# A decoder block's expert stage: first table of tiles in three pieces, earlier pads, down product one tile sooner

## The reference, cut to what matters

```
x = x + attn(norm(x))            # returns its input plus the attention: 16 heads of 8
x = x + xattn(norm(x), ctx, ctx) # 16 heads of 64, rotary, causal window of 32
x = x + ffn(norm(x))             # below

logits = x_ @ router.T ; idx = argmax(logits)      # 8 experts, one per row
y  = down[idx] @ (silu(gate[idx] @ x_) * (up[idx] @ x_))
ys = shared expert, for every row
return y + ys
```

## Time and profile before

| what | value |
|---|---|
| median of three runs | 772.91 us |
| the profiled execution | 773.4 us |
| its span in the trace | 771.3 us |
| PE busy, share of the span | 740.5 us, 96% |
| DVE (VectorE) | 544.2 us, 71% |
| ACT (ScalarE) | 534.7 us, 69% |
| POOL (GpSimd) | 525.7 us, 68% |
| mean granted clock of PE | 0.986 |

### The profile page before, as it was taken

How to read it: one execution, slowest core, us unless ns; L and a number is a source line. 1 busy time by engine, 2 the same in 40 slices (tenths; PEclk the granted TensorE clock), 3 DMA queues, 4 the chain that set the end, 5 groups by cost and what they waited for, 6 DMA issues and landing times.

```text
span 771.3 us, 31550 instructions
## 1 busy us (share of the span) xinstructions
PE 740.5 (96%) x11799; PEld 603.4 (78%) x11799; DVE 544.2 (71%) x1401; ACT 534.7 (69%) x1943; POOL 525.7 (68%) x857
## 2 busy tenths in 40 slices
PE   7999999999999999999999999999999989998894
PEld 6778878888888888787888888888888868776563
DVE  3467777777777777688777777777777777657463
ACT  2367777777777777777777777777777757774362
POOL 5466677677777777777777777777777756474554
PEclk9999999999999999999999999999999989999898
DMA  6000000111111000000000000000000003015420
GB/s 242 9 9 9 29 27 28 34 38 37 38 37 38 13 17 25 23 17 24 24 24 24 24 17 14 17 17 17 17 17 10 11 1 97 10 52 182 119 82 21
DMA packets 23539, 28.74 MB, mean 37 GB/s; under 512 B 3416, under 2 KB 19676, under 8 KB 23392
## 3 DMA queue, kind: packets, MB, share of 16 engines
q1 hardware_dynamic: 19888, 18.55, 8.0%
q0 software_dynamic: 2784, 6.56, 2.5%
q10 hardware_dynamic: 720, 1.63, 0.6%
HBM read 16.82 MB, written 10.35 MB: 35 GB/s over the span
## 4 chain that ended last, share of the span: by engine, by line
PE 91%; DVE 2%; ACT 2%; issue 2%; DMA 1%; SPq 0%; POOL 0%; POOLq 0%; ACTq 0%; DVEq 0%
PE P L277 8%; PE P L312 8%; PE P L287 8%; PE P L297 7%; PE P L353 7%; PE P L339 6%; PE P L325 5%; PE P L229 5%; PE P L212 4%; PE P L371 4%; PE P L244 4%; PE P L418 4%; PE P L379 3%; PE P L252 2%; PE P L342 1%
## 5 line engine op out<-in xcount | busy, mean ns | idle before, releaser
L857 ACT ACTIVATE PX<-P,mx 128x128 f32<-128x128 f32 x512 | 183.6, 393 | 27.7 <-DVE mx L590 27.7
L1027 POOL TENSOR_TENSOR PX<-PX,mx 128x512 f32<-128x512 f32 x128 | 130.5, 1041 | 36.5 <-DVE mx L595 36.5
L590 DVE TENSOR_REDUCE mx<-P 128x4 f32<-128x512 f32 x128 | 81.2, 678 | 93.5 <-PE P L312 93.5
L857 ACT ACTIVATION_READ_ACCUMULATOR PX<-P,mx 128x1 f32 x512 | 119.3, 233 | 0.0
L866 ACT ACTIVATE PT<-P 128x512 f32<-128x512 f32 x128 | 70.0, 597 | 64.5 <-PE P L325 64.5
L973 POOL TENSOR_SCALAR st<-st 128x1 f32<-128x1 f32 x96 | 22.0, 229 | 105.9 <-DVE st L498 99.6
L1022 POOL TENSOR_TENSOR rq<-rq,tq 128x1024 f32<-128x1024 f32 x32 | 75.6, 2363 | 25.9 <-DVE rq L554 25.9
L529 DVE TENSOR_REDUCE nmf<-P 128x4 f32<-128x512 f32 x128 | 79.5, 683 | 13.8 <-PE P L212 13.8
L821 ACT ACTIVATE PS<-P 128x512 f32<-128x512 f32 x128 | 66.1, 602 | 28.4 <-PE P L233 28.4
L1017 POOL TENSOR_TENSOR rk<-rk,tk 128x1024 f32<-128x1024 f32 x32 | 75.5, 2360 | 1.1 <-DVE tk L554 1.1
L277 PE MATMUL P<-wvT,cxT 128*128 128x512 f32 x128 | 72.2, 646 | 0.0
(11 more groups left out here) (156 smaller groups left out, 1828.7 us busy)
## 6 DMA issues: line engine op xcount, KB each, us to landing
xrow<-z_xs SPq DMA_DIRECT2D x39, 136.0 KB, 2.1
ew<-in_ew SPq DMA_DIRECT2D x9, 384.0 KB, 3.3
z_xs<-c SPq DMA_DIRECT2D x8, 272.0 KB
x<-in_x SPq DMA_DIRECT2D x32, 64.0 KB, 1.7
cxT<-in_ctxT SPq DMA_DIRECT2D x31, 64.0 KB, 1.8
z_xs<-c SPq DMA_DIRECT2D x8, 136.0 KB, 3.1
out<-yst,xrow POOLq DMA_INDIRECT x39, 2.3
wk<-in_wk SPq DMA_DIRECT2D x1, 512.0 KB, 4.5
```

Source lines behind the costliest of these rows:

```text
L590: dve.tensor_reduce(mx[b % 3][:, 0, r, :], v3(bank(f"ds{r}")), AX.X, ALU.max, negate=True).then_inc(S["v_dm"][r], 1)
L857: t = act.activation(PX[(4 * b + r) % 6][:, c, :], p[:, c * 128:c * 128 + 128], ACT.Exp, bias=m[:, 0, r, c:c + 1], scale=1.0, accum_out=m[ ...
L1027: pool.tensor_tensor(X[:, :, :], X[:, :, :], mx[b % 3][:, 2, r, :].rearrange("p (h a) -> p h a", a=1).to_broadcast([128, 4, 128]), ALU.mul ...
```

## The change

Five things are changed.

- The table is cut into three functions. `table_sums` has the count of tiles and the sums, `table_experts` the experts and exg, `table_rows` the first rows and exr. For c = 0 only the sums stay in f_pos; table_experts(0) runs one period later between r_q3 and r_q1 (f_experts, s - 8), table_rows(0) later in that period between the d_max and r_k1 (f_rows). For c = 1 all three follow each other in f_pos.
- The number of tiles is now had by rounding: a large number is added, at which float32 has steps of 128, and taken off again, two operations on 8 numbers. The minimum is part of exg's operation, and in the second table the last addition part of exr's.
- The pads use the counts of batch 29 and are 384 rows long; batch 30's scatter waits for them. SP's first_r is called in the period of the last piece.
- In the last loop the down product and VectorE's sum are those of tile j - 3, and the loops are one iteration shorter.
- WARM has 13 idle products for ('nmt', 2) instead of 16.

```diff
--- before.py
+++ after.py
@@ -37,7 +37,7 @@
             xr0=4, xr1=5, xr2=2, xr3=2, xrt0=4, xrt1=5, xt0=3, xt1=0, xt2=2, xt3=7, xtt0=0, xy0=0, xy1=3, xy2=7,
             xy3=1, xyt0=6, xyt1=7)
 WARM = {('a', 0): 36, ('a', 1): 14, ('nmt', 0): 43, ('kE', 1): 13, ('cnt', 0): 13, ('qO', 0): 9, ('ds0', 0): 22,
-        ('cnt', 1): 19, ('nmt', 2): 16}
+        ('cnt', 1): 19, ('nmt', 2): 13}
 S0, PERIODS = 27, 45
 
 
@@ -383,7 +383,7 @@
 
             def f_pos(b):
                 until = [(S["v_pse"], b + 1)]
-                if b == NB - 2:
+                if b == NB - 3:
                     until.append((S["v_pad"], 1))
                 if b + 1 in (FIRST[1], NB):
                     until.append((S["v_cnt"], chunk(b) + 1))
@@ -478,11 +478,11 @@
                 batch(d_t, s - 5, 0)
                 batch(b_s, s - 3)
                 tile(x_hT, s - 35, 0)
-            for j in range(TILE0[1], NT + 4):
+            for j in range(TILE0[1], NT + 3):
                 last(x_tr, j)
                 last(x_hT, j - 3)
                 last(x_up, j - 1)
-                last(x_dn, j - 4)
+                last(x_dn, j - 3)
 
         @block.vector
         def _(dve):
@@ -642,29 +642,29 @@
                 dve.tensor_tensor(f[:, 0:8], bank("pos")[:, 0:8], OH[:, b, :], ALU.mult).then_inc(S["v_own"], 1)
                 dve.wait_ge(S["v_own"], own())
                 dve.tensor_reduce(f[:, 8:9], f[:, 0:8], AX.X, ALU.add).then_inc(S["v_pse"], 1)
-                if b == NB - 2:
+                if b == NB - 3:
                     dve.scalar_tensor_tensor(out=padr[:, :], in0=experts, scalar=float(128 * CAP), in1=bank("pos")[:, 8:16],
                                              op0=ALU.mult, op1=ALU.add).then_inc(S["v_pad"], 1)
                 if b + 1 in (FIRST[1], NB):
                     dve.tensor_copy(cnt[:, 0:8], bank("pos")[:, 8:16]).then_inc(S["v_cnt"], 1)
-                    tile_table(chunk(b))
-
-
-
-
-            def tile_table(c):
-                t0, T = TILE0[c], TILES[c]
-                n = [CHUNKS[0], NB][c]
-                own_tiles, incl, w = cnt[:, 8:16], cnt[:, 16:24], cnt[:, 24:32]
-
-                done, after, upto, before = cnt[:, 32:40], cnt[:, 33:41], cnt[:, 41:49], cnt[:, 40:48]
-                cm = cmpb[:, 0:8 * n].rearrange("p (e j) -> p e j", e=NE)
+                    table_sums(chunk(b))
+                if b + 1 == NB:
+                    table_experts(1)
+                    table_rows(1)
+
+
+
+
+            own_tiles, incl, w = cnt[:, 8:16], cnt[:, 16:24], cnt[:, 24:32]
+
+            done, after, upto, before = cnt[:, 32:40], cnt[:, 33:41], cnt[:, 41:49], cnt[:, 40:48]
+
+            def table_sums(c):
+
                 dve.wait_ge(S["v_cnt"], c + 1)
-                dve.tensor_tensor(cm, cnt[:, 0:8].rearrange("p (e a) -> p e a", a=1).to_broadcast([128, NE, n]),
-                                  steps[:, 1 - c:1 - c + n].rearrange("p (a j) -> p a j", a=1).to_broadcast([128, NE, n]),
-                                  [ALU.is_ge, ALU.is_gt][c]).then_inc(S["v_own"], 1)
+                dve.tensor_scalar(own_tiles, cnt[:, 0:8], [-63.5, 63.5][c], 1.5 * 2.0 ** 30, ALU.add, ALU.add).then_inc(S["v_own"], 1)
                 dve.wait_ge(S["v_own"], own())
-                dve.tensor_reduce(own_tiles, cm, AX.X, ALU.add).then_inc(S["v_own"], 1)
+                dve.tensor_scalar(own_tiles, own_tiles, -1.5 * 2.0 ** 30, 1.0 / 128, ALU.add, ALU.mult).then_inc(S["v_own"], 1)
                 dve.wait_ge(S["v_own"], own())
                 if c == 1:
                     dve.tensor_tensor(own_tiles, own_tiles, done, ALU.subtract).then_inc(S["v_own"], 1)
@@ -672,12 +672,16 @@
                 c2 = cmpb[:, 0:64].rearrange("p (e f) -> p e f", e=NE)
                 dve.tensor_tensor(c2, own_tiles.rearrange("p (a f) -> p a f", a=1).to_broadcast([128, NE, NE]),
                                   tri[:, :, :], ALU.mult).then_inc(S["v_own"], 1)
-                dve.wait_ge(S["v_own"], own())
-                dve.tensor_reduce(incl, c2, AX.X, ALU.add).then_inc(S["v_own"], 1)
                 dve.tensor_scalar(w, own_tiles, -1.0, float(CAP), ALU.mult, ALU.add).then_inc(S["v_own"], 1)
                 own()
                 dve.wait_ge(S["v_own"], own())
+                dve.tensor_reduce(incl, c2, AX.X, ALU.add).then_inc(S["v_own"], 1)
+                own()
+
+            def table_experts(c):
+                t0, T = TILE0[c], TILES[c]
                 c3 = cmpb[:, 0:8 * T].rearrange("p (j e) -> p j e", e=NE)
+                dve.wait_ge(S["v_own"], mine[0])
                 dve.tensor_tensor(c3, incl.rearrange("p (a e) -> p a e", a=1).to_broadcast([128, T, NE]),
                                   tiles[:, 0:T].rearrange("p (j a) -> p j a", a=1).to_broadcast([128, T, NE]),
                                   ALU.is_le).then_inc(S["v_own"], 1)
@@ -697,21 +701,32 @@
                 dve.tensor_reduce(exf[:, 0:T], c3, AX.X, ALU.add).then_inc(S["v_own"], 1)
                 own()
                 dve.wait_ge(S["v_own"], own())
-                dve.tensor_scalar(exf[:, 0:T], exf[:, 0:T], 7.0, None, ALU.min).then_inc(S["v_own"], 1)
                 dve.tensor_tensor(c3, c3, w.rearrange("p (a e) -> p a e", a=1).to_broadcast([128, T, NE]),
                                   ALU.mult).then_inc(S["v_own"], 1)
+                dve.tensor_scalar(exg[:, t0:t0 + T], exf[:, 0:T], 7.0, float(EW), ALU.min, ALU.mult).then_inc(S["v_ex"], 1)
                 own()
-                dve.wait_ge(S["v_own"], own())
-                dve.tensor_scalar(exg[:, t0:t0 + T], exf[:, 0:T], float(EW), None, ALU.mult).then_inc(S["v_ex"], 1)
+
+            def table_rows(c):
+                t0, T = TILE0[c], TILES[c]
+                c3 = cmpb[:, 0:8 * T].rearrange("p (j e) -> p j e", e=NE)
+                dve.wait_ge(S["v_own"], mine[0])
                 dve.tensor_reduce(exf[:, MOST:MOST + T], c3, AX.X, ALU.add).then_inc(S["v_own"], 1)
                 dve.wait_ge(S["v_own"], own())
                 dve.tensor_tensor(exf[:, MOST:MOST + T], exf[:, MOST:MOST + T], tiles[:, 0:T], ALU.add).then_inc(S["v_own"], 1)
                 dve.wait_ge(S["v_own"], own())
                 if c == 1:
-                    dve.tensor_scalar(exf[:, MOST:MOST + T], exf[:, MOST:MOST + T], cnt[:, 32:33], None,
-                                      ALU.add).then_inc(S["v_own"], 1)
-                    dve.wait_ge(S["v_own"], own())
-                dve.tensor_scalar(exr[:, t0:t0 + T], exf[:, MOST:MOST + T], 128.0, None, ALU.mult).then_inc(S["v_ex"], 1)
+                    dve.tensor_scalar(exr[:, t0:t0 + T], exf[:, MOST:MOST + T], cnt[:, 32:33], 128.0, ALU.add,
+                                      ALU.mult).then_inc(S["v_ex"], 1)
+                else:
+                    dve.tensor_scalar(exr[:, t0:t0 + T], exf[:, MOST:MOST + T], 128.0, None, ALU.mult).then_inc(S["v_ex"], 1)
+
+            def f_experts(b):
+                if b + 1 == FIRST[1]:
+                    table_experts(0)
+
+            def f_rows(b):
+                if b + 1 == FIRST[1]:
+                    table_rows(0)
 
             def x_gate(j):
                 T, p = xth[j % 3], bank(xbank("xg", j))
@@ -740,6 +755,7 @@
                 tile(x_gate, s - 36, 3)
                 batch(b_max, s - 4, 3)
                 batch(r_q3, s - 5)
+                batch(f_experts, s - 8)
                 batch(r_q1, s - 5)
                 batch(d_ox, s - 6, 0)
                 tile(x_y, s - 36, 1)
@@ -752,6 +768,7 @@
                 batch(d_max, s - 5, 3)
                 batch(d_max, s - 5, 0)
                 batch(d_max, s - 5, 2)
+                batch(f_rows, s - 8)
                 batch(r_k1, s - 3)
                 tile(x_gate, s - 35, 0)
                 batch(f_y, s - 7)
@@ -766,9 +783,9 @@
                 batch(f_pos, s - 7)
                 batch(b_x1, s - 4)
                 batch(d_ri, s - 5, 2)
-            for j in range(TILE0[1], NT + 4):
+            for j in range(TILE0[1], NT + 3):
                 last(x_gate, j - 1)
-                last(x_y, j - 4)
+                last(x_y, j - 3)
 
         @block.scalar
         def _(act):
@@ -1050,7 +1067,7 @@
                 pool.wait_ge(S["p_pos"], b + 1)
                 pool.wait_ge(S["s_er"], b + 1)
                 pool.wait_ge(S["v_fy"], b + 1)
-                if b == NB - 1:
+                if b == NB - 2:
                     pool.wait_ge(S["d_pad"], 16 * NE)
                 pool.indirect_dma_start(out=A["z_xs"], out_offset=bass.IndirectOffsetOnAxis(ap=pos[:, b:b + 1], axis=0),
                                         in_=er[b % 4][:, :], in_offset=None).then_inc(S["d_sc"][b % 4], 16)
@@ -1116,12 +1133,12 @@
 
 
             def pads(b):
-                if b == NB - 2:
+                if b == NB - 3:
                     sp.wait_ge(S["v_pad"], 1)
                     for e in range(NE):
-                        row = sp.value_load(padr[0:1, e:e + 1], min_val=128 * CAP * e, max_val=128 * (CAP * e + CAP - 2))
```

(7 more changed lines are left out.)

## The result

The changed kernel takes 768.88 us, the median of six runs (767.43 to 770.27); six runs of the kernel before beside it gave 772.70 (770.91 to 773.63). The ratio is 0.9953, 95% interval [0.9937, 0.9968]: 3.8 us faster, where 6.25 were forecast. The profiled execution took 768.65 us, its span is 766.5 us and its mean granted clock 0.994.

What follows compares the result with a forecast made beforehand. TensorE, busy throughout ordinary periods, was taken as the bound, so only its waits and low clock counted. -4.5 - 0.9 + 0.1 - 0.8 - 0.15 (warm-up) = -6.25 us gave 766.7 us; range 763.5 to 769.0.

Steps and rivals of the forecast that it cites:

- First table, -4.5: First table's period: -5.78 for the old excess, +0.4 wait at L212, +0.9 stall from the middle piece; bounds -5.0 to -3.6.
- Two things of PE hang on it: Middle piece between r_q3 and r_q1: delays L312 through POOL's rq and L304 through the second oX; 0.9 us stall.
- 5.78 more: First table's period before the change: 25.97 us instead of an ordinary 20.19, for the same products.
- Second table, -0.9, clock as before: Second table shortened from 3.98 to 3.1 us, PE's gap from 3.32 to 2.4; gain 0.9 us (0.7 to 1.0).
- I take it that it falls: Behind the second table's gap of 2.4 us: the clock still falls, as 2.4 lies nearer 2.95 than 0.7.
- rival A: Second table's gap: the clock holds through it, 2.4 us more gained, 764.3 us; chance 0.27.
- Down product, -0.8: Last loop, product three tiles behind: last send at 763.4 instead of 764.21; bounds 0.8 lost to 0.8 gained.
- I take no stall: Last loop's down product behind ACT's copy: 0.27 us just enough; 0 to 0.05 us per tile, 0 to 0.8 in all.
- rival B: Last loop: no slack, 16 iterations at 0.05, last sum ends the chain, not POOL; 0.8 to 1.6 us more; chance 0.15.
- Pads, +0.1: PE's wait for VectorE's reading of the counts: the pad's 8-element operation adds 0.1 us (0 to 0.2).
- rival C: Loads of tile 15 or 16 held behind the larger pads, making the kernel slower than before, 774 us; chance 0.03.
- PE doesn't wait for that scatter's tiles: Batch 31's scatter: POOL's 4.26 us wait before it goes, but counts 0 us for PE.

## Why the prediction was wrong in size

- **First table, -4.5.** Right in mechanism and nearly in size: 25.97 to 21.67 is -4.30 between the profiled executions. L212 waits 0.35 (0.4 forecast); the middle piece costs 0.97 (run with it later) where 0.9 was forecast, though not at L304 or L312. "Two things of PE hang on it" left out a third, the bank of L339, which r_q1 reads; that the size came out all the same is luck. What was mis-sized is the starting point: "5.78 more" is one trace. The two other traces of this period on chips of this kind have 25.86 and 24.75, the last with only 3.4 us at half clock instead of 6.8. The mean gain is 25.53 - 21.69 = 3.84.
- **Second table, -0.9, clock as before.** The gap shrank by 0.79 (3.32 to 2.53). "I take it that it falls" and rival A (it holds, 0.27) were each right in half of the traces: the clock held in two of four traces of the change and fell in two, which is 15.90 or 17.0 us to tile 20. So the price of a fall is 1.1 us here and not A's 2.4, and the trace that was forecast from had a dear one (18.81 with 6.8 us at half speed, 17.88 with 3.4, 16.82 with none, in a gap of 3.40). The mean gain is 1.4.
- **Down product, -0.8.** This step failed. "I take no stall", with 0.05 us for each tile as the upper bound, met 0.07, since I took the 0.27 us behind ACT's copy for slack. It was used: the weights of L433 went in ahead, under L418, and waiting for a copy of the same iteration takes that away, since the load can't start before 0.24 us behind the copy. In the pair of traces that differ by this edit alone, moving the product gave 0.50 - 1.18 = -0.7, nearly the 0.8 forecast for the sends, and the stalls took 1.0: the net is +0.3, off by 1.1. The stall is rival B's, with its price (0.8 to 1.6), to which I gave 0.15; its other half, that the last sum ends the chain and not POOL, isn't in the trace, where the last two sends of the change still follow 1.28 and 1.31 us behind the one before.
- **The start of the last loop.** This step was missing: the forecast has no clock fall there. PE's timeline after, behind the last batch:

```profile
720.49 0.48 PE L433 MATMUL P<-ew,xhT 128*128 x2 [0.67 <-ACT xhT L924]
...
721.67 0.33 PE L407 MATMUL P<-c,xrow 128*128 128x128 f32 x1 [0.37 <-ACT xsT L912]
722.51 1.42 PE L418 MATMUL P<-ew,xsT 128*128 x2 [0.52 <-ACT xsT L912]
```

Three waits, 1.56 us within 2.7, and the clock was at 0.50 from 723.2. Their like are in every kernel here, also in the one with the second table in pieces, which kept its clock. It fell here in all four traces of the change and in one of three of the kernel before, at 1.0 to 1.5 us a time (30.6 beside 29.59, 29.22, 29.50 and 29.65 beside 28.14). It is also in the run of the change with the old last loop, so the down product isn't its cause. Mean: +0.7. What brings the fall isn't shown: the same three waits stand in traces that kept their clock. A fall at the second table doesn't protect this place, since two traces of the change fell at both.
- **Pads, +0.1.** PE's wait at the counts and SP's and POOL's part, three timelines of after:

```profile
683.81 0.72 PE L325 MATMUL P<-c,PX 64*128 64x64 f32 x16 [0.53 <-DVE padr L646]
```

```profile
684.32 10.04 SPq L1140 DMA_DIRECT2D z_xs<-c  x8
```

```profile
699.39 1.11 POOL L1072 DMA_INDIRECT z_xs<-er,pos  x1 [1.54 <-DMA z_xs<-c]
```

0.53 instead of 0.31, so +0.2, the upper bound; the eight issues 10.04 instead of 9.49 us for half as much again in bytes, and no product waits for the loads of tiles 15 to 18, so rival C had nothing to stand on; POOL waits 1.54 us instead of 4.26, and for batch 30's scatter now. What I valued at 0, "PE doesn't wait for that scatter's tiles", was right in this kernel and in one trace each way worth 0.84 us once the second gap had gone.
- **Warm-up, -0.15.** Not measurable: 1.0001 on the kernel before.

In sum, with means over the traces: -3.84 at the first table; -1.4 to tile 20 (0.8 the gap, 0.6 clock); +1.45 and -1.17 for the down product; +0.7 the clock in the last loop: -4.2. Against the forecast of -6.25 the down product's stall took 1.1, the clock at the start of the last loop 0.7 and the dear first trace 0.65, while the second table gave 0.5 more; the rest is pads and warm-up. The difference from -4.2 to the measured -3.8 is less than what the early periods vary by from trace to trace (5.7 to 10.0).

On the clock the Trainium skill (TensorE: Matmul & The Clock Gate, Part 1: The HAM clock gate) has a free-running window, and these traces agree as far as they go: in the kernel before a gap of 3.40 us at the second table brought the clock down in one trace and left it in another. Over all traces here, PE's gaps of 2.9 to 3.4 us at a table were followed by a fall in 11 of 12 cases and gaps of 2.3 to 2.5 us in 5 of 11.

## What to carry to other kernels

Price a clock fall from several traces of the same kernel and book it as a chance: here one program's period went from 24.75 to 25.97 us by it. Where the bounding engine shows no idle time, a wait can still take away a weight load that ran ahead; look at where the load stands in the timeline, not only at when its operand is ready. And cut a serial computation into the places where its engine waits for the bounding one: 4.1 us came with moving the second table's pieces (a part of it clock that held), and nothing measurable from the shorter sums with the first table in one piece.

## What the runs showed of the hardware

The same program takes 772 us on two chips and 804 to 807 us on two others, at the same granted clock in its ordinary periods. In the trace of 806.0 us against that of 771.3, 20 us of the difference are 1.0 us in nearly every period up to the first table. Most of the rest stands in the four periods behind it, where the clock falls. The row that carries 26 us is L312 (64 products of 32 rows per batch), which has more busy time and more waits marked issue. On the faster chips only some early periods are longer. No edit here changed that, and why a chip is of the one kind or the other stays open.
